# A fused layer norm, latent attention and feed-forward kernel: other first stage, larger PV groups, Newton steps for the root

## What is computed

```python
xn = _layernorm(x)                                  # (x - mean) / sqrt(var + 1e-5)
q = einsum('bld,dhk->blhk', xn, Wq)                 # 16 heads of 64
latent = einsum('bld,dc->blc', xn, Wkv_down)        # 64 wide
k = einsum('blc,chk->blhk', latent, Wk_up)
v = einsum('blc,chk->blhk', latent, Wv_up)
attn = softmax(causal(einsum('bqhd,bkhd->bhqk', q, k) / sqrt(64)))
y = einsum('bhqk,bkhd->bqhd', attn, v)
attention = einsum('bqhd,hdo->bqo', y, Wout)
ffn = tanh(xn @ weight @ aux_weight1 @ aux_weight2 + bias)
out = x + attention + ffn
```

## Time and profile before

| | us |
|---|---|
| median of 3 runs | 2208.31 (2206.73 to 2210.28) |
| profiled execution | 2213.74, of which the span of the trace is 2212.0 |
| first stage, up to the first matmul of the body | 77.3 |
| PE, DVE, POOL, ACT busy | 2113.0, 1501.2, 1313.6, 1062.1 |

### The profile page before, as it was taken

One profiled execution on the slowest core, in us unless ns is written; L12 is line 12 of the kernel. 1 busy time (PEld: TensorE's weight loads), 2 busy tenths in 40 slices (PEclk: granted clock), 3 DMA queues, 4 the chain that ended last, 5 costly groups with the idle time before them and its releaser, 6 DMA issues.

```text
span 2212.0 us, 32578 instructions
## 1 busy us (share of the span) xinstructions
PE 2113.0 (96%) x9912; PEld 1279.8 (58%) x9912; DVE 1501.2 (68%) x3695; ACT 1062.1 (48%) x1970; POOL 1313.6 (59%) x1163
## 2 busy tenths in 40 slices
PE   6999999999999999999999999999999999999997
PEld 4555556655565555555556555555556555666554
DVE  4677657776677766777667766767667776577662
ACT  3445454554544444445544444545444454545543
POOL 0366665666666565665556655566655666556665
PEclk8999999999999999999999999999999999999999
DMA  3011111110111111111111110111111111111111
GB/s 104 19 32 49 32 42 44 35 54 25 47 42 40 45 28 46 40 53 40 28 47 35 54 42 28 47 37 49 39 30 49 40 49 33 38 49 30 40 30 39
DMA packets 66999, 91.18 MB, mean 41 GB/s; under 512 B 12304, under 2 KB 33680, under 8 KB 66832
## 3 DMA queue, kind: packets, MB, share of 16 engines
q1 hardware_dynamic: 66832, 89.11, 14.4%
HBM read 45.55 MB, written 8.91 MB: 25 GB/s over the span
## 4 chain that ended last, share of the span: by engine, by line
PE 74%; DVE 12%; DMA 3%; ACT 3%; issue 3%; SPq 1%; POOL 0%; DVEq 0%; ACTq 0%
PE ps L858 22%; PE ps L872 11%; PE ps L841 10%; PE ps L905 9%; PE ps L844 9%; PE ps L812 8%; DVE ps L1083 3%; PE ps L895 3%; DVE maxima L1088 3%; ACT q_hi L1059 2%; DMA q_hi<-q_hi 1%; DVE xn L1165 1%; DVE norm L1106 1%; ACT probs L1002 1%; DMA norm<-recips 1%
## 5 line engine op out<-in xcount | busy, mean ns | idle before, releaser
L1218 POOL TENSOR_TENSOR p_sum<-p_sum,probs 128x512 f32<-128x512 f32 x672 | 864.5, 1305 | 356.8 <-ACT probs L1002 353.7
L1002 ACT ACTIVATE probs<-ps 128x512 f32<-128x512 f32 x1152 | 670.1, 596 | 641.1 <-PE ps L844 597.5
L1083 DVE CUSTOM_DVE_ANT_0 ps<-ps,causal 128x256 f32<-128x256 f32 (+3 forms) x1024 | 492.7, 503 | 276.2 <-PE ps L872 269.6
L858 PE MATMUL ps<-probs,latent 128*64 128x512 f32 x2304 | 558.9, 612 | 0.0
L841 PE MATMUL ps<-q_hi,k_hilo 128*128 128x512 f32 x1152 | 513.8, 446 | 18.5 <-ACT probs L1002 14.9
L872 PE MATMUL ps<-k_hilo,q_hi 128*128 128x512 f32 (+3 forms) x1536 | 473.8, 375 | 24.8 <-DVE maxima L1088 14.6
L844 PE MATMUL ps<-q_lo,k_ones 65*128 65x512 f32 x1152 | 460.9, 400 | 0.0
L1088 DVE TENSOR_REDUCE maxima<-ps 128x1 f32<-128x512 f32 x512 | 351.3, 686 | 118.6 <-PE ps L872 116.5
L1206 POOL TENSOR_SCALAR_AFFINE_SELECT probs<-probs 128x512 f32<-128x512 f32 x256 | 165.9, 652 | 416.1 <-ACT probs L1002 415.5
L872 PEld LDWEIGHTS ps<-k_hilo,q_hi 128*128 128x128 f32 x1536 | 277.9, 190 | 197.2 <-issue 64.8
L1218 POOL TENSOR_TENSOR p_sum<-probs 128x512 f32<-128x512 f32 x224 | 286.2, 1289 | 105.5 <-ACT probs L1002 104.1
(11 more groups left out here) (91 smaller groups left out, 1497.7 us busy)
## 6 DMA issues: line engine op xcount, KB each, us to landing
q_hi<-q_hi SPq DMA_DIRECT2D x256, 128.0 KB, 2.3
norm<-recips SPq DMA_DIRECT2D x256, 128.0 KB, 2.9
x_in<-in_L_attn_x_bld SPq DMA_DIRECT2D x8, 1024.0 KB, 5.5
out_x<-acc SPq DMA_DIRECT2D x64, 128.0 KB, 1.7
q_lo<-rows SPq DMA_DIRECT2D x128, 4.0 KB
rows<-norm SPq DMA_DIRECT2D x128, 4.0 KB
recips<-rows SPq DMA_DIRECT2D x128, 4.0 KB
probs<-in_L_attn_Wq SPq DMA_DIRECT2D x1, 1024.0 KB, 8.0
```

The lines of the kernel that those rows point to most:

```text
L858: last = nc.tensor.matmul(y_bank[g * LATENT:(g + 1) * LATENT, :], latent[par][:, key_block(unit, s), :], probs[:, t % PT_SLOTS, g * BANK:( ...
L1002: nc.scalar.activation(probs[:, t % PT_SLOTS, g * BANK:(g + 1) * BANK], st_bank[(2 * t + g) % ST_BANKS], ACT.Exp).then_inc(exp_done, 1)
L1083: nc.vector.tensor_tensor_reduce(bank, bank, causal[:, BANK - w:BANK], 1.0, LOWEST, ALU.add, ALU.max, maxima[:, unit % 4, h:h + 1]).then_i ...
L1218: nc.gpsimd.tensor_tensor(sums, other, probs[:, slot, part], ALU.add).then_inc(pool_done, 1)
```

## The change

- **First stage.** The folding of wqk is cut in two (`fold wqk 0`, `fold wqk 1`) and lies around the products that make the keys; PE no longer waits for all constants before its first transposes; all eight groups of x are turned before the first fold; the low part of a query follows one pair later; the eight maxima of unit 0 are mixed with the transposes and products of the other weights. Banks are renumbered for that (0 becomes 7).
- **AHEAD** is 1: the 16 chunks of unit 1, and its MT, move from the first stage to the start of the body. `LEAD` = 12 keeps the due times where they were for all later units.
- **Planner.** `BATCH` 4 for 3, `PT_SLOTS` 7 for 6, `SUM_SLOTS` 2 for 3; three prices for tile changes; other durations, above all for the landing of DMAs.
- **Layer norm.** The root on ACT and the five operations after it go. DVE shifts the bits of var + epsilon, subtracts from a constant and makes three Newton steps of three operations each: 12 small operations in a row where there were one and five.
- **Maxima.** The two halves of a unit's maxima lie side by side, and one `tensor_reduce` over them into `joined` replaces the `tensor_tensor` of `L1094`.

```diff
-AHEAD = 2
-ST_BANKS, PT_SLOTS, Y_SLOTS, SUM_SLOTS = 2, 6, 3, 3
+AHEAD = 1
+ST_BANKS, PT_SLOTS, Y_SLOTS, SUM_SLOTS = 2, 7, 3, 2
...
-LANDING = {"Q": 2600, "MT": 2200, "X": 6000, "RG": 2200, "RO": 2200, "RB": 3200}
-NARROW = ("PV", "R")
-INTO_NARROW, OUT_OF_NARROW = 140, 180
-BATCH = 3
+LANDING = {"Q": 2900, "MT": 2300, "X": 6000, "RG": 2600, "RO": 2200, "RB": 4300}
+WIDTHS = {"PV": 64, "R": 32}
+INTO_PAIRS, INTO_QUADS, OUT_OF_TILES = 155, 100, 205
+BATCH = 4
 SOON = 60
+LEAD = 12
...
-        self.max_at = list(itertools.accumulate([c[3] / (OCTET * P) for c in self.maxima], initial=0))
+        self.max_at = list(itertools.accumulate([c[3] / (OCTET * P) for c in self.maxima],
+                                                initial=sum(block_of(u) + 1 for u in range(AHEAD)) - LEAD))
...
-    plan += [("LN1", 0), ("LN2", 0), ("W", "constants"), ("LN3", 0)]
+    plan += [("LN1", 0)]
     plan += [("LN4", (0, k)) for k in range(2)]
...
+    plan += [("W", "fold wqk 0"), *two_parts("K", (0, 0)), ("KL", (0, 0))]
+    plan += [*two_parts("K", (0, 1)), ("KL", (0, 1)), ("W", "fold wqk 1"), ("KN", 0)]
     for j in range(PAIRS):
...
+    plan += maxima[:2] + [("QL", (0, PAIRS - 1)), maxima[2], ("W", "turn others")] + maxima[3:5]
+    plan += [("W", "fold aux")] + maxima[5:7] + [("W", "fold wvo"), maxima[7]]
+    return plan + [("MT", 0), ("W", "fold wff")]
...
-                        nc.vector.tensor_tensor(maxima[:, unit % 4, :], maxima[:, unit % 4, :],
-                                                maxima0[:, unit % 4, :],
-                                                ALU.max).then_inc(max_joined, 1)
+                        nc.vector.tensor_reduce(joined[:, unit % 4, :], maxima[:, unit % 4, :, :],
+                                                AX.X, ALU.max).then_inc(max_joined, 1)
...
+                    for n in range(3):
+                        chained(nc.vector.tensor_tensor(square, last, last, ALU.mult))
+                        chained(nc.vector.scalar_tensor_tensor(
+                            out=scale, in0=square, scalar=-0.5, in1=var, op0=ALU.mult,
+                            op1=ALU.mult))
+                        chained(nc.vector.scalar_tensor_tensor(
+                            out=guess, in0=scale, scalar=1.5, in1=last, op0=ALU.add,
+                            op1=ALU.mult))
+                        last = guess
```

More of the change, by code:

```diff
@@ L28 @@
 F32R = mybir.dt.float32r
+I32 = mybir.dt.int32
 P = 128
@@ L182, in flush @@
             elif kind == "LN1":
-                self.after(self.run("DVE", when, DVE_TIME[kind]), "LN2", key)
-            elif kind == "LN2":
-                self.after(self.run("ACT", when, ACT_TIME[kind]), "LN3", key)
-            elif kind == "LN3":
                 end = self.run("DVE", when, DVE_TIME[kind])
@@ L277, in place_max @@
         whole = k0 + w == (block_of(u) + 1) * P
-        dve = (w + 80) / 0.96 if whole else 605
+        dve = (w + 100) / 0.96 if whole else 610
         last = h == OCTET - 1 and whole
-        dve += 300 if last and k0 else 0
+        dve += 200 if last and k0 else 0
         self.max_free.append(self.run("DVE", end, (dve, dve + (180 if whole else 130))))
@@ L701, in fold_on_pe @@
                                              for j in (2 * n, 2 * n + 1) for c in range(C)])
+            elif what == "turn wk":
                 transposes(wk_bank, [wk_in[:, j * P:(j + 1) * P] for j in range(HEADS // 2)])
[L703 removed]
+            elif what in ("fold wqk 0", "fold wqk 1"):
                 pe.wait_ge(w_copied, 5)
[L706 to L714 removed]
+                c = int(what[-1])
+                for g in range(2):
+                    r = g * HD
+                    for j in range(HEADS // 2):
+                        last = nc.tensor.matmul(
+                            wq_banks[2 * c + g][:, j * LATENT:(j + 1) * LATENT],
+                            wqT[r:r + HD, j, c * P:(c + 1) * P], wkT[r:r + HD, j, :],
+                            start=True, stop=True)
+                    last.then_inc(w_full, 1)
@@ L743, in fold_on_act @@
                     copied(n + 1, wqT_flat[:, n * BANK:(n + 1) * BANK], wq_banks[n])
+            elif what == "turn wk":
                 copied(5, acc_flat[:, 0:512], wk_bank)
-            elif what == "fold wqk":
-                for n in range(4):
+            elif what in ("fold wqk 0", "fold wqk 1"):
+                for n in range(2 * int(what[-1]), 2 * int(what[-1]) + 2):
                     copied(6 + n, *wqk_part(wqk_hi, n), scale=HD ** -0.5)
@@ L750, in fold_on_act @@
                 copied(10, acc_flat[:, 512:1024], ps[:, 5, :])
-                copied(11, norm[:, 0, :], ps[:, 0, :])
+                copied(11, norm[:, 0, :], ps[:, 7, :])
                 copied(12, acc_flat[:, 1536:2048], ps[:, 1, :])
+            elif what == "fold aux":
+                copied(13, acc_flat[:, 1024:1536], ps[:, 6, :])
             elif what == "fold wvo":
-                copied(13, acc_flat[:, 1024:1536], ps[:, 6, :])
-                for n, bank in enumerate((5, 0, 1)):
+                for n, bank in enumerate((5, 7, 1)):
                     copied(14 + n, wvo_part(n), ps[:, bank, :])
@@ L768, in fold_on_dve @@
         def fold_on_dve(dve, what):
-            if what == "constants":
+            both = [slice(r * LATENT, (r + 1) * LATENT) for r in range(2)]
+            if what == "casts":
                 dve.wait_ge(wkv_loaded, 16)
                 dve.wait_ge(consts_made, 7)
-                both = [slice(r * LATENT, (r + 1) * LATENT) for r in range(2)]
                 for cols in both:
@@ L777, in fold_on_dve @@
                 nc.vector.memset(ones[:, :], 1.0).then_inc(w_split, 1)
+            elif what == "residuals":
+                dve.wait_ge(w_split, 2)
+                for cols in both:
+                    nc.vector.tensor_tensor(wkv_lo[:, :, cols], wkv_in,
+                                            wkv_hi[:, :, cols].bitcast(F32),
+                                            ALU.subtract).then_inc(w_split, 1)
                 for i in range(2):
@@ L783, in fold_on_dve @@
                             causal[64:65, :], 0.0, 1.0, ALU.mult, ALU.add).then_inc(w_split, 1)
-                dve.wait_ge(w_split, 2)
-                for cols in both:
-                    nc.vector.tensor_tensor(wkv_lo[:, :, cols], wkv_in,
-                                            wkv_hi[:, :, cols].bitcast(F32),
-                                            ALU.subtract).then_inc(w_split, 1)
-            elif what == "fold wqk":
-                for n in range(4):
+            elif what in ("fold wqk 0", "fold wqk 1"):
+                for n in range(2 * int(what[-1]), 2 * int(what[-1]) + 2):
                     lo, bank = wqk_part(wqk_lo, n)
@@ L878, in tensor_program @@
                     p1_ready()
+                    if count.has("W", "fold wvo"):
+                        pe.wait_ge(w_copied, 15)
                     if block_of(key) < 4:
@@ L931, in tensor_program @@
                     if kind == "K0":
+                        if count.has("W", "residuals"):
+                            pe.wait_ge(w_split, CONSTANTS)
                         p0_ready()
@@ L955, in tensor_program @@
                     if kind == "Q0":
-                        if count.has("W", "fold wqk"):
+                        if count.has("W", "fold wqk 1"):
                             pe.wait_ge(w_split, CONSTANTS + 4)
```

108 lines of the change are left out of this document (43 added, 65 removed).

## The result

The changed kernel takes 2116.7 us (median of 4 runs, 2116.4 to 2124.8) against 2209.3 of before on the same chip: ratio 0.958, 95% interval 0.956 to 0.960. The forecast was 2145 with a range from 2118; the time lies 28 us under the one and 1.3 under the other, nearest to the rival by which the corrected durations do more (2112). The profiled execution took 2116.38 us, a span of 2114.6.

The account below looks back on a forecast made before the run. PE's own list was taken to bound the kernel (busy 96%). From 2213.7 the terms -23 + 6 - 14 - 12 - 10 - 10 - 7 + 5 + 1.5 gave 2150.2, less 5.4 for the median 2145 us; range 2118 to 2179.

Parts of the forecast that it names:

- the rival by which the corrected durations do more: Whole launch: larger savings on neighbours and projections, clock and stall whole, Newton chain free; 2112 us, chance 10%.
- First stage: Launch start: reordered transposes, folds and maxima let the body start earlier, -23 us (bounds -18 and -27).
- near 54: Sign at the end of the first stage: the body's first matmul comes near 54 us instead of 77.3.
- Unit 1's maxima: Moved to the body's start: 3.8 us of PE work plus 2.3 of waiting, +6 us (bounds +4 and +10).
- Fewer changes of width: PE's whole order: fewer switches between full width and PV tiles, 0.33 us a visit, -14 us (bounds -11 and -17).
- Stall and clock: Body's layer norms: PE's stall goes, -10 us, and half of 20.4 us lost to the low clock, -10.
- sign of no gap over 0.5 us: At the layer norm PE would show no gap over 0.5 us.
- Newton chain: DVE at each layer norm: 12 small operations for 6, 0.7 us a batch reaching PE, +5 us (bounds 0 and +65).
- neighbours: PE in the body: fewer waits where MAX follows MAX or half-step follows half-step, -12 us (bounds 0 and -25).
- projections: PE's projections idle 13.3 us for the normalized y; corrected landings save half, -7 us (bounds 0 and -12).
- third rival: Layer norms: POOL's additions hold the chain's two-input DVE operations, PE waits 65 to 70 us, 2247 us; chance 4%.
- Tail and median: Launch end: last gathers queue behind other DMA waits, +1.5 us; median of runs taken 5.4 below the profiled execution.

Follow-up runs that it names:

- a_lead13: The changed kernel with maxima due 13 steps ahead where it has 12, so the planner deals another order; 2163.3 us, ratio 0.980.
- a_slots6: The changed kernel, still with groups of four, but 6 probability slots and 3 sum buffers as before; 2116.1 us, ratio 0.958.
- b_copyroot: The kernel before, same order, with ACT copying where it took the layer norm's root, so the table loads there go; 2208.7 us, ratio 0.999.
- a_group3: The changed kernel with groups of three, 6 probability slots and 3 sum buffers as before; 2168.6 us, ratio 0.981.
- a_sqrt: The changed kernel with the layer norm of before (root on ACT, its small operations and planner entries); 2172.1 us, ratio 0.985.
- b_grouptimes: The kernel before with groups of four, their prices and the corrected durations; 2180.8 us, ratio 0.986.
- a_oldtimes: The changed kernel with the planner's old durations (DVE, landings, R); 2162.0 us, ratio 0.979.
- b_groupnewton: The kernel before with groups of four, their prices and the Newton steps; 2191.5 us, ratio 0.993.
- a_redraw1: The changed kernel with the planner's price for going from full width to pairs 150 ns for 155, giving another order; 2117.1 us, ratio 0.959.
- a_newton1: The changed kernel in its own order with one Newton step at each layer norm for three; 2115.5 us, ratio 0.959.
- a_newton6: The changed kernel in its own order with six Newton steps at each layer norm for three; 2158.2 us, ratio 0.977.
- a_best2: The changed kernel with several planner numbers moved (groups up to 5, maxima due 10 steps ahead, thresholds, longer Newton chain entry); 2076.7 us, ratio 0.941.

## Why the prediction was right and wrong

**First stage: right in size, in part by luck.** -24.2 for -23, the body's first matmul at 53.1 for "near 54". But the stage's length goes with the clock in it, for which the forecast had no term. Behind the very same first stage the body starts at 51.3 in `a_lead13`, with nothing at 1.2 GHz, and at 59.0 in `a_slots6`, with 17 us at 1.2 GHz; the change has 3.4, before had 27.3, and `b_copyroot`, in before's order, starts at 82.6 with 34. An agreement to 1 us is closer than two executions agree. Unit 1's maxima: PE's 3.8 us came; the 2.3 of waiting put beside them hardly did.

**Fewer changes of width: right.** The list fell by 11 us (18 by the other sorting), forecast -14 + 3.8. `a_group3` confirms the price: its list is 17 us longer (18 by the other sorting) with 262 - 210 = 52 returns more, 0.33 us each.

**Stall and clock: right place for this order, wrong cause, half of the clock.** The forecast let the stall go because the table loads go and the chain comes to stand behind a PV group. The second is so in the new order; of the first `b_copyroot` shows that the loads never held PE. Nor did the stall go; it was cut up. PE of the changed kernel at the third batch's layer norm (timeline):

```profile
439.53 1.14 PE L874 MATMUL ps<-k_hilo,q_hi 128*128 128x128 f32 x3 [0.34 <-DVE maxima L1093]
...
446.88 0.50 PE L814 MATMUL ps<-xT_hi,wqk_hi 128*128 128x512 f32 x1 [1.03 <-DVE q_lo L1196]
...
452.29 0.50 PE L874 MATMUL ps<-k_hilo,q_hi 128*128 128x512 f32 x1 [0.58 <-DVE maxima L1088]
```

Three short holds within 13 us stand where one of 1.20 was, 1.95 us together, so the -10 for the stall did not come as less idle time there, and the forecast's sign of no gap over 0.5 us failed. None of the three is followed by a fall, and the 20.4 us of slow clock, of which the forecast counted half, are all saved.

**Waits: twice the forecast.** -12, -10 and -7, less the 5 of the Newton chain and the 2.3 at the body's start, were -22; the measured difference is -41 (-35 by the other sorting). By instruction the waits fell for maxima from 63 to 40, for half-steps from 58 to 44 and for the turns of maxima from 17 to 3; for the first projection of a unit they stayed (21 and 22), and for the first queries they rose from 3 to 14. The step of the prediction that failed is this sum: neighbours -12, stall -10, projections -7 and half of the clock, -10, each worked out as if it did not matter to it which other parts were there. In place of -22 and -10 the trace has -41 and -21, and the runs show why no sum of separate terms could give it: durations, Newton steps and grouping alone are worth -31, +9 and +20 us of body, which adds to -2, while together they give -72, unit 1's maxima included. From two parts to three the body falls by 47 to 52 us, whichever comes last. About 20 of that is the clock, of which every pair loses 15 to 25 us: `a_group3`, `a_sqrt` and `b_grouptimes` at five to seven of the layer norms, `a_oldtimes` and `b_groupnewton` nearly all elsewhere. The rest is waiting. The count of MAX behind MAX as a measure of waits is refuted by `a_redraw1`. Projections waiting for the normalized y, put at -7, did not get less (15.0 us after, 13.3 before). The rival that came nearest in number, 2112, had the whole clock and a free Newton chain right and the projections wrong.

**Newton chain: somewhat longer on DVE, next to nothing on PE.** The twelve small operations of a batch are 1.7 us more of DVE than the six of before, for +1.3. They last 0.17 us, but two in each batch of the body last 0.49 to 0.65. These do not lie under POOL's additions but under its shorter clears above the diagonal, as here (timelines of POOL and DVE):

```profile
437.89 0.64 POOL L1213 TENSOR_SCALAR_AFFINE_SELECT probs<-probs 128x512 f32<-128x512 f32 x1 [0.61 <-ACT probs L1010]
```
```profile
437.93 0.62 DVE L1158 SCALAR_TENSOR_TENSOR ln<-ln 128x8 f32<-128x8 f32 x1
```

`L1157`, `L1158` and `L1161` exceed 0.167 by 5.5 us over eight batches, 0.7 a batch. The forecast's 0.7 was for what reaches PE, so that the two figures agree is chance (groups by line and shape):

```profile
L1158 DVE SCALAR_TENSOR_TENSOR ln<-ln 128x8 f32<-128x8 f32 x24 | 6.6, 277 | 0.8
L1157 DVE TENSOR_TENSOR ln<-ln 128x8 f32<-128x8 f32 x16 | 5.1, 316 | 0.5
L1161 DVE SCALAR_TENSOR_TENSOR ln<-ln,bits 128x8 f32<-128x8 f32 x8 | 1.8, 227 | 0.3
```

`a_newton1` shows that hardly any of it reaches PE (1 us, inside the interval, where 5 were charged), and `a_newton6`, whose longer chain runs into the additions, that the third rival's mechanism is real and begins soon beyond.

**Tail and median.** From the start of the last half-step to the end of the span it is 21.5 us before and 22.7 after, +1.3 for +1.5; but `b_copyroot`, in before's order, has 22.6, so this is within the scatter of executions. All but the last three matmuls of it are counted in the body above; behind those the difference is -0.7. The 5.4 us taken off for the median belong to the scatter of before, whose profiled execution lies near its upper end; that of the change lies 0.4 under its median. That the subtraction brought the forecast nearer to the time is chance.

Counted from 2145: -19 for waits, -11 for the clock, -1 first stage, -2 behind the body and +6 for the median give 2118, against 2116.7 measured.

**Left open.** Why these three parts together give an order whose holds are short all along the body, while any two don't, is not explained beyond the places shown. Nor is what decides whether a hold brings a fall: 4.26 us did at all seven layer norms of `a_newton6`, 2.8 us at six of seven in `a_best2`, and the longest hold of the change ahead of 2095 us, 1.61 us at 802.7, did not; `b_copyroot` has the same 1.19 us at 479.28 as before without one, while before has one 2.3 us behind its 1.20.

## What to carry to other kernels

Where a greedy planner writes a static order, the parts of a change don't add: count only what is on the bounding engine's own list, and give the waits one common range, as wide as the share of waiting in the body, not a sum of small terms. Look first for the holds of PE that every batch repeats, wherever they lie (the layer norm, the next keys and the row of maxima in these kernels), since a hold there can be paid a second time in the clock behind it. Keep the planner's landings true, because an engine parked early at a DMA's wait holds everything queued behind it, and try its few numbers on the chip: moving them gave another 40 us on top of the change.

## What was not expected of the hardware

Removing 15 of 16 table loads of 1.28 us each moved the time by nothing (0.999, 0.998 to 1.001). One pair of POOL additions stretched two operations of 0.17 us to 1.26 and 1.18, and in the same kernel `L1172`, with one large input in SBUF, lasts 2.42 us for two under the next pair of additions and 0.73 for two without:

```profile
455.49 0.73 DVE L1172 TENSOR_SCALAR xn<-x_in,mean_var,ln 128x256 f32<-128x256 f32 x2
...
456.95 2.42 DVE L1172 TENSOR_SCALAR xn<-x_in,mean_var,ln 128x256 f32<-128x256 f32 x2
```

The join written as `tensor_reduce` over one tile takes 170 ns where the `tensor_tensor` over two took 463 on average. That average is a mixture: 30 of the 64 began under an addition of POOL and lasted 0.79 us on average and up to 1.15; of the other 34 all but one lasted 0.17. Of the 64 `tensor_reduce` 18 began under such an addition in the change and 42 in `a_best2`, and none lasted over 0.172 us. It is the cheapest way found here round such holds.
